# Sort lanes of 126 edges, base and rank in one product, runs of 7 in the first pass

## The reference

```python
x = emb[x_ids]
def layer(x_prev, W_a, b_a, W_b, b_b):                 # three times
    msg = vals[:, None] * x_prev[col]
    h = segment_sum(msg, row, num_segments=N)
    z = (h + x_prev) @ W_a.T + b_a + h * x_prev @ W_b.T + b_b
    return where(z >= 0, z, 0.2 * z)
return concatenate((x, x1, x2, x3), axis=1)            # 12500 x 512
```

## Time and profile before

| what | value |
|---|---|
| median of three runs | 11672.61 us |
| the profiled execution | 11676.03 us |
| its span on the core | 11674.3 us |
| mean granted TensorE clock | 0.861 |
| busy: PE / VectorE / ScalarE / GpSimd | 9811.1 / 8287.8 / 3867.5 / 5876.3 us |
| first and last scatter issue of pass 0 | 363.7 and 2011.9 us |
| first and last scatter issue of pass 1 | 2431.4 and 4129.8 us |

### The profile page before, as it was taken

How to read it: one execution, slowest core, us unless ns; L and a number is a source line. 1 busy time by engine, 2 the same in 40 slices (tenths; PEclk the granted TensorE clock), 3 DMA queues, 4 the chain that set the end, 5 groups by cost and what they waited for, 6 DMA issues and landing times.

```text
span 11674.3 us, 234500 instructions
## 1 busy us (share of the span) xinstructions
PE 9811.1 (84%) x66108; PEld 8442.8 (72%) x66109; DVE 8287.8 (71%) x13757; ACT 3867.5 (33%) x12047; POOL 5876.3 (50%) x4395
## 2 busy tenths in 40 slices
PE   6898997689999947998888789988787899878877
PEld 4677776467777736997676679986666799867666
DVE  6877776777777746776666667766666677766666
ACT  0566665046666602662000036630000256400001
POOL 7577776047777710003777710027777300177774
PEclk8666666766666657999999999999999999999999
DMA  2111111011111194998666779986666799966666
GB/s 78 17 4 4 4 4 15 5 3 4 4 4 4 4 26 158 343 341 256 190 191 187 184 190 343 346 275 190 186 190 187 158 338 346 303 187 192 190 188 139
DMA packets 1150180, 1744.93 MB, mean 149 GB/s; under 512 B 472915, under 2 KB 524183, under 8 KB 1149494
## 3 DMA queue, kind: packets, MB, share of 16 engines
q0 software_dynamic: 430880, 809.77, 30.8%
q1 hardware_dynamic: 719254, 934.66, 27.1%
HBM read 990.83 MB, written 752.96 MB: 149 GB/s over the span
## 4 chain that ended last, share of the span: by engine, by line
DMA 24%; issue 17%; PE 15%; DVE 3%; POOL 2%; ACT 2%; POOLq 1%; SPq 0%; DVEq 0%; ACTq 0%
DMA messages<-work 13%; DMA work<-messages,work 11%; PE ps L885 6%; PE ps L876 6%; POOL work L499 2%; ACT work L658 2%; DVE work L1248 2%; PE ps L856 2%; PE ps L893 1%; PE ps L913 1%; PE ps L914 1%; POOLq L497 0%; PE ps L903 0%; SPq L576 0%; POOLq L493 0%
## 5 line engine op out<-in xcount | busy, mean ns | idle before, releaser
L499 POOL DMA_INDIRECT work<-messages,work x3000 | 3250.7, 1084 | 4194.6 <-issue 4022.7
L885 PE MATMUL ps<-work 128*128 128x125 f32 x24000 | 3394.6, 288 | 910.4 <-DVE work L1248 878.4
L885 PEld LDWEIGHTS ps<-work 128*128 128x128 f32 x24000 | 2911.5, 193 | 1393.5 <-DVE work L1248 1379.8
L475 POOL DMA_INDIRECT sorted_edges<-stage,run_idx x1270 | 2420.2, 1906 | 1456.4 <-DMA sorted_edges<-stage,run_idx 535.4
L1248 DVE SCALAR_TENSOR_TENSOR work<-work,iota_p 128x500 f32<-128x500 f32 x3000 | 2219.9, 740 | 1295.7 <-DMA work<-messages,work 1281.3
L876 PE MATMUL ps<-xb,work 125*128 x21504 | 2458.0, 276 | 149.7 <-DVE work L1220 83.0
L876 PEld LDWEIGHTS ps<-xb,work 125*128 125x128 f32 x21504 | 2423.7, 192 | 183.9 <-issue 183.5
L769 PEld LDWEIGHTS ps<-hT 128*128 128x128 f32 x12700 | 2187.4, 272 | 392.5 <-issue 371.4
L769 PE MATMUL ps<-hT 128*128 128x80 f32 x12700 | 2190.7, 357 | 286.6 <-ACT hT L617 217.7
L658 ACT ACTIVATE work<-ps,work 128x128 f32<-128x128 f32 x5376 | 1511.4, 371 | 1394.1 <-PE ps L876 730.7
L614 ACT ACTIVATE hT<-iota_p,place 128x128 f32<-128x128 f32 x4826 | 1437.2, 387 | 403.4 <-DVE place L1057 381.1
(11 more groups left out here) (199 smaller groups left out, 3843.1 us busy)
## 6 DMA issues: line engine op xcount, KB each, us to landing
messages<-work SPq DMA_DIRECT2D x2688, 256.0 KB, 6.2
work<-slot_cols SPq DMA_DIRECT2D x672, 256.0 KB, 6.0
work<-messages,work POOLq DMA_INDIRECT x3000, 3.8
sorted_edges<-stage,run_idx POOLq DMA_INDIRECT x1270, 3.2
out_x<-xb SPq DMA_DIRECT2D x150, 125.0 KB
work<-lane_places SPq DMA_DIRECT2D x508, 5.5 KB, 3.4
out_x<-xb SPq DMA_DIRECT2D x4, 1562.5 KB
sorted_edges<-hT SPq DMA_DIRECT2D x4, 906.0 KB
```

The lines of the kernel that those rows point to most:

```text
L475: pool.indirect_dma_start(out=sorted_edges[p], out_offset=bass.IndirectOffsetOnAxis(ap=run_idx[:, q, k:k + 1], axis=0), in_=stage[:, q, k ...
L499: pool.indirect_dma_start(out=ck[:, n, :], out_offset=None, in_=messages, in_offset=bass.IndirectOffsetOnAxis(ap=idx[:, h * BU + n:h * BU ...
L885: last = t.matmul(part[n], ck[:, n, j * D:(j + 1) * D], sel[:, n % SELB, j, :], start=j == 0, stop=j == CH - 1)
```

## The change

Lanes have 126 edges (`LN`), on partitions 0 to 125. Pass 0 then has 3175 lanes and 127 windows, pass 1 has 3275 lanes and 131 windows. Partitions 126 and 127 of `oh` hold the two base rows of the window, to which `load_rows` writes; rows 126 and 127 of `after_b` are ones. So `rank` is five products with all 128 rows, and the five two-row products are gone. The instructions that work on edges take 126 partitions; shapes along the free dimension are as they were, apart from pass 0, where runs have 7 records (56 bytes) in place of 8, and a partition 35 slots in place of 40: L1065 and L1071 have 875 elements per partition, the order product 2 x 35 columns. The number of scatter DMAs per window (five, each of 128 runs) stays. The edges do not fill 126 partitions evenly: 125 partitions hold 3175 edges, the last 3125. Each of the three edge arrays therefore comes in three DMAs (partitions 0 to 111, 112 to 124, 125), after three small fills of the unused columns. In the tables, lanes times 126 stand where lanes times 128 stood; there is no other new work. The core of the diff:

```diff
-COLS = E // P
-TILES1 = E // P + NB
+LN = P - 2
+COLS = -(-E // LN)
+TILES1 = COLS + NB
-RUN = 8
+RUN = [7, 8]
+SLOTS = [RUNS * r for r in RUN]
-        oh = wb[:, 2 * OH0:2 * OH0 + 2 * OHW].rearrange("p (q x) -> p q x", q=2)
-        rows = wb[0:2, 2 * ROWS0:2 * ROWS0 + 2 * ROWW].rearrange("h (q x) -> h q x", q=2)
+        oh = wb[:, 2 * OH0:2 * OH0 + 2 * ROWW].rearrange("p (q x) -> p q x", q=2)
+        rows = [oh[LN + h:LN + h + 1, :, :] for h in range(2)]
+            g.affine_select(out=after_b[:, :], in_=after_b[:, :], compare_op=ALU.is_gt, fill=1.0,
+                            base=LN, pattern=[[0, P]], channel_multiplier=-1).then_inc(const_ready, 1)
-                sp.dma_start(dst, src.rearrange("(p c) -> p c", p=P)).then_inc(edges_in, DMA)
+                for p0, p1, w in ((0, 112, COLS), (112, FULLP, COLS), (FULLP, LN, LEFT)):
+                    if k == 0 and p0 == 0:
+                        sp.wait_ge(unused_set, 3)
+                    sp.dma_start(dst[p0:p1, 0:w], src[...].rearrange("(p c) -> p c", c=w)).then_inc(edges_in, DMA)
                 for k in range(BANKS):
-                    t.matmul(ps[:, k, 0:BANKW], ones_b[0:2, :], rows[:, q, k * BANKW:(k + 1) * BANKW], start=True, stop=False,
-                             skip_group_check=True)
-                for k in range(BANKS):
-                    last = t.matmul(ps[:, k, 0:BANKW], after_b[:, :], oh[:, q, k * BANKW:(k + 1) * BANKW], start=False, stop=True,
-                                    skip_group_check=True)
+                    last = t.matmul(ps[:, k, 0:BANKW], after_b[:, :], oh[:, q, k * BANKW:(k + 1) * BANKW], start=True, stop=True)
                 for k in range(LANES):
-                    last = t.matmul(ps[:, 6 + q, 0:2 * SLOTS], to_part[q][:, k, :],
-                                    moved[q][:, k, :, :].rearrange("p f c -> p (f c)"), start=k == 0, stop=k == LANES - 1)
+                    last = t.matmul(ps[:, 6 + q, 0:2 * SLOTS[p]], to_part[q][:, k, :],
+                                    moved[p][q][:, k, :, :].rearrange("p f c -> p (f c)"), start=k == 0, stop=k == LANES - 1)
-                v.tensor_tensor(in_slot[q], slot[:, :, None].to_broadcast([P, LANES, SLOTS]),
+                v.tensor_tensor(in_slot[p][q], slot[:, :, None].to_broadcast([LN, LANES, slots]),
```

More of the change, by code:

```diff
@@ L48 @@
 WMAX = max(WINDOWS)
-RUN = 8
 RUNS = 5
-SLOTS = RUN * RUNS
-assert LANES * P + NB * 2 * (RUN - 1) <= P * SLOTS
+RUN = [7, 8]
+SLOTS = [RUNS * r for r in RUN]
+SMAX = max(SLOTS)
+for k in range(2):
+    assert LANES * LN + NB * 2 * (RUN[k] - 1) <= P * SLOTS[k]
 BANKB = 20
@@ L91 @@
 assert ABODIES * ZC >= N and ABODIES * ZC == 12544 and TB == 1000 and GROUPS % AU == 0 and AU == CB * BATCH and AU % MR == 0
-UNITS = [P, GE]
-DUMPS = [LT * P // RUN, SLOTS2 // RUN]
+UNITS = [LN, GE]
+DUMPS = [LT * LN // RUN[0], SLOTS2 // RUN[1]]
+assert FULLP == LN - 1 and LT * LN % RUN[0] == 0 and LN % RUN[0] == 0 and GE % RUN[1] == 0
 SPARE = RUNS * P
+SROWS = [-(-(d + SPARE) // (4 * P)) * 4 * P for d in DUMPS]
 ZW = SLOTS2 * 2 // P // 4 + 32
@@ L118, in dram @@
             return nc.dram_tensor(name, shape, dt, kind="Internal").ap()
-        sorted_edges = [dram(f"sorted_edges{k}", [DUMPS[k] + SPARE, RUN * 2]) for k in range(2)]
+        sorted_edges = [dram(f"sorted_edges{k}", [SROWS[k], RUN[k] * 2]) for k in range(2)]
         lane_places = dram("lane_places", [2, NBD, LT], BF16)
@@ L156, in graph_layers @@
         place = sb("place", [P, 2, 4, LANES])
-        stage = sb("stage", [P, 2, SLOTS, 2])
+        stage = sb("stage", [P, 2, SMAX, 2])
         run_idx = sb("run_idx", [P, 2, RUNS], I32)
@@ L192, in graph_layers @@
         assert IR0 + SPARE <= 20560
-        hot = [hb[:, r * LT:(r + 1) * LT] for r in range(HR)]
+        hot = [hb[0:LN, r * LT:(r + 1) * LT] for r in range(HR)]
         lane_at = hT[0:NBD, 0:LT]
@@ L371, in keep_turned @@
                     eng.wait_ge(turned, m + 1)
[L372 removed]
+                    copy(rows_[:, g0:g1, :], ps[0:LN, m % 8, 0:(g1 - g0) * P].rearrange("p (g t) -> p g t", t=P),
                          *how).then_inc(turned_kept[f], 1)
@@ L436, in _ @@
             count(iota_l[:, :], [[P, TABW]], mul=1)
-            count(iota_s[:, :], [[1, SLOTS]], base_=int(BIG))
+            count(iota_s[:, :], [[1, SMAX]], base_=int(BIG))
             count(iota_pk[:, :], [[1, RUNS]], mul=RUNS)
@@ L516, in _ @@
             for p in range(2):
-                size = (DUMPS[p] + SPARE) * RUN * 2 // P // 4
+                size = SROWS[p] * RUN[p] * 2 // P // 4
                 assert size <= ZW
@@ L950, in counting @@
                 link(v.tensor_tensor_scan(dst, one, one, value_, ALU.mult, ALU.add))
+            for k in range(3):
+                v.memset(unused[k], 0.0 if k else 1.0).then_inc(unused_set, 1)
             v.memset(zeros, 0.0).then_inc(zeros_ready, 1)
@@ L990, in run_tables @@
             def run_tables(p):
-                W, U, unit = WINDOWS[p], USED[p], float(UNITS[p])
+                W, U, unit, run = WINDOWS[p], USED[p], float(UNITS[p]), RUN[p]
                 tab = lambda name: window_tab(name, W)
@@ L1047, in window @@
                 n = WOFF[p] + w
-                at, raised, part_of, slot = [place[:, q, k, :] for k in range(4)]
+                at, raised, part_of, slot = [place[0:LN, q, k, :] for k in range(4)]
+                slots = SLOTS[p]
                 dve.wait_ge(rank_ready, n + 1)
```

102 lines of the change are left out of this document (54 added, 48 removed).

## The result

| | before | after |
|---|---|---|
| median of 4 runs, us | 11679.63 (11668.24 to 11694.44) | 11759.47 (11750.18 to 11772.2) |
| profiled execution, us | 11676.03 | 11750.18 |
| its span, us | 11674.3 | 11748.4 |

The changed kernel is 0.7% slower: ratio 1.0068, 95% interval 1.0055 to 1.0082. That answers the forecast in sign and nearly in size: 11731 us was forecast, the measured median lies 28 us above it.

A forecast was written before the change was run, and what follows sets the result against it. GpSimd's serial chain of five scatter issues and a landing bounds the sort. Terms 52.8 - 9 + 4 + 6 + 2 + 3 = +59 us gave median 11731 us; range 11680 to 11785 (8 in 10: 11550 to 11870).

The forecast's parts named there:

- Part 1: Sort windows: five two-row products less counted at 0 us, hidden by GpSimd's chain; L1041's place leaves 13.2 us a window.
- part 3: Pass 0, runs of 7 records: issue, landing and shorter L1065 and L1071 counted at 0 us; landing bounds -37 and +190.
- Part 2: Both sort passes: two windows more in each, 4 x 13.2 = +52.8 us, on the path.
- rival D: Pass 0: 56-byte runs land later, +0.5 us a window, +64 us, 11795 us; chance 0.08.
- rival C: Pass 0: shorter L1065 and L1071 come off the chain, -55 us, total +4, 11676 us, no change; chance 0.05.
- Part 4: Before each pass's first scatter: first rank and first order product get shorter, 2 passes x 4.5 = -9 us.
- Part 5: Tables and counting: table steps +4 us, counting +6 us, full-width VectorE instructions between the passes +2 us.
- Part 6: Start: six more load issues of 0.41 us each and three fills of about 0.7 us, +3 us on the path.
- A: Sort: order product ends earlier, L1041 slips into GpSimd's wait, 12.5 us a window, -120 us, 11552 us; chance 0.27.
- B: Sort at the low clock: L1041 locks onto the scatter issues, 13.8 us a window, +154 us, 11885 us; chance 0.16.
- A's extreme form: Sort: PE is the bound, the whole 1.95 us a window goes, -440 us, 11232 us; chance 0.04.
- The sign against C: In the steady sort, the issue at 1149.00 lies wholly inside two L1071 yet takes 1.67 us, 0.13 more than shortest.

The follow-up runs named there:

- e1: Changed kernel with each window's five rank products done twice; 12283.46 us, ratio 1.0040 to the kernel before on the same chip.
- e6: Kernel before with four scatter issues per window in place of five; 11251.58 us, ratio 0.9634 to the kernel before.
- e9: Changed kernel with one-hot block numbers from PSUM and four scatter issues per window; 11353.67 us, ratio 0.9345 to the kernel before, same chip.
- e10: Kernel before with one-hot block numbers from PSUM and four scatter issues per window, run again; 11503.66 us, ratio 0.9473 to the kernel before, same chip.
- e2: Changed kernel with the one-hot's block numbers read from PSUM rather than SBUF; 11947.34 us, ratio 0.9775 to the kernel before, same chip.
- e3: Kernel before with the one-hot's block numbers read from PSUM rather than SBUF; 11910.16 us, ratio 0.9739 to the kernel before, same chip.
- e8: Kernel before with its three edge loads cut into nine; 11685.76 us in one run, against 11673.4 us for the kernel before.
- e7: Kernel before with one-hot block numbers from PSUM and four scatter issues per window; 11061.22 us, ratio 0.9465 to the kernel before.
- e4: Changed kernel with ids, weights and biases loaded ahead of the nine edge loads; 12305.39 us in one run, kernel before 12227.96 us.

## Why the prediction was right

- **What bounds the sort.** GpSimd's chain of issues and landing, not the busier TensorE. Right, and shown from both sides: e1 (TensorE loaded again, no loss) and e6 (one issue less, 3.7% gained).
- **Part 1, the removed products at nothing.** Right in the sum, and in part by luck. The pass periods did not fall, and e1 gives the work back for nothing over both passes. But in pass 0 the removed products moved L1055 onto the issues: it holds them 1.50 us a window in place of 1.21, some 39 us more over the pass, and e1 takes that back (1.18). The shorter f32 instructions of part 3 hid it: they gave 35 us back in the same pass. In pass 1 the one-hot's share fell in the kernel after and in e1 alike, so there it is not TensorE's doing. The cover was real and finite: in e9 against e10, where it is gone, the same edit brings 150 us.
- **Part 1, where L1041 falls.** The prediction took the mean of 13.2 us out of 11.3 to 14.0, as it stood before. Measured are 13.27 and 13.20; in pass 0 the choice held since two shifts cancelled. That L1041 is what stretches a window is shown by e2 and e3.
- **Part 2, four windows.** Forecast 52.8 us. The passes took 63.0 us longer, of which 52.8 are the windows (4 x 13.2); the other 10 are the slightly longer pauses between scatters, 8 of them in pass 0 (34.5 - 26.4).
- **Part 3, 56 bytes for 64.** Right at 0 for the landing. GpSimd's waits for the landing are 2.47 us each in pass 0 (276.5 us, 112 times), where rows have 56 bytes, and 2.49 in pass 1 (288.4, 116), where they have 64. That rejects rival D. The shorter L1065 and L1071 were not hidden, though, as the prediction had them: see rival C.
- **Part 4, the fill.** 4.5 us a pass forecast, 4.6 measured in pass 0; for pass 1 no row tells it apart from the tables.
- **Part 5, tables and counting.** 12 us forecast in all; 5.0 measured ahead of pass 0, and between the passes +3.5 with the fill of pass 1 in it, so 8 without it if that fill saved as much: 13. The start of the first rank differs by 5.8 us between the kernel before and e3, so this is no sharp test.
- **Part 6, the loads. This is the term that was mis-sized.** "Six more issues of 0.41 us each" priced the issuing alone, +3 us. The landing took 10.1 us longer (e8: 10.6 us by the cut alone). With the drift of part 2 it makes up the distance: 59 forecast, 74.1 in the two spans; the layers gave 2.9 us back.
- **The rivals.** A and B are out at their prices in the kernel as it is: the period went neither to 12.5 nor to 13.8 us. B's side remark, that less work brings TensorE the lower clock, did hold in pass 0 (0.65 to 0.60) and not in pass 1 (0.66 to 0.67). A's extreme form, TensorE as the bound, comes true only with the chain shortened (e7, and e9 against e10). C's mechanism is at work, though its outcome is not seen: the f32 instructions held the issues of pass 0 for 73 us and now hold them for 38, a gain of 35 where C counted 55, and the one-hot took as much back.
- **The sign against C was misread.** The issue at 1149.00 does not lie wholly inside the two L1071: it ends at 1150.67, they at 1150.36. And what counts is what was running at its start, the first L1071, which ended at 1149.25: 1.54 + 0.25 - 0.12 = 1.67 us, as measured. By the Trainium skill, SBUF — State Buffer, section "Who interferes with whom", a VectorE instruction with two SBUF inputs contends with a GpSimd instruction that reads SBUF, and the order of issue decides who blocks. The traces agree, for bf16 and f32 alike: in e9 the issue at 1007.83 starts inside L1078, which ends at 1008.61, and takes 2.19 us (1.54 + 0.78 - 0.12 = 2.20), though more such instructions follow beside it. The same section infers that a tensor_tensor does not stall the making of DMA descriptors; the 3.73 us beside the one-hot speak against that.
- **Three readings of rows.** ScalarE's wait "longer than 1210 us" came to 1229, but by the four windows more; TensorE's gain went into its own waits for the Relu. TensorE's share in pass 0 "near 78%" does not follow from its own terms: 1.95 of 13.2 us are 15 points, which from 86% gives some 72%. Measured are 82%, ten points off, as the lower clock took part of the saving back (and 77% in pass 1, where the clock stayed). And the 418 us of waits for a stage both fall at the start of pass 1, not at the starts of both passes.

## What to carry to other kernels

Before taking work off the busiest engine, ask who is waited for: an engine that is 86% busy but whose result is never waited for has nothing to give, and a change that pays for its relief with more rounds of the serial chain loses just those rounds. Keep such an edit at hand all the same; when the chain has been shortened, it is worth its price (here +0.7% alone, -1.3% behind the two other edits). When one engine holds up another, do not judge by what overlaps, but by which instruction was already running when the other started: that told the length of nearly every issue here. And price a load by its landing, with the DMA rate of the stretch, not by the time its issue takes.

## What the runs showed of the hardware

- The same compare-to-one-hot of 128 x 2500 bf16 takes 2.76 us on VectorE with its second input in SBUF or in PSUM. With SBUF it stretches an indirect DMA's issue on GpSimd from 1.54 to about 3.9 us, with PSUM an issue wholly inside it takes 1.54 us (e2): 1.2 to 1.4 us in every window of 13.2.
- An indirect DMA's issue on GpSimd is held by a VectorE instruction with two SBUF inputs, bf16 or f32, only if that was running when the issue started, and then for its remaining time less 0.12 us (2552 of 2560 issues of the kernels before and after within 0.1 us). One that starts later costs the issue nothing (the issue at 1008.07).
- Three loads of 128 partitions cut into nine (112, 13 and 3 partitions, same bytes) let VectorE start 10.6 us later, at mostly 200 to 280 GB/s instead of 400 to 440, with the DMA engines shown as busy (e8).
- More work went with a higher granted clock of TensorE: with the rank products done twice, most slices of the sort stand at 0.7 in place of 0.6 on the same chip (e1, e4). In the change itself less work went with a lower clock in pass 0 (0.65 to 0.60) and not in pass 1 (0.66 to 0.67). Of 457 us of products removed, 257 us of busy time were saved; some 42 us of the rest are the four windows more.
- A float32 product of 64 columns takes TensorE as long as one of 80 at 1.2 GHz, 0.22 us (e6).
